# A vision tower on one Trainium2 core: value matmuls grouped, the weighing merged, PSUM banks and step orders reassigned, and the second norm applied by GpSimd

## What is computed

```
tokens  = patches(14 x 14) @ W.T + b           # 196 tokens of 128
h       = concat(token, tokens) + pos          # S = 197 rows
x       = layernorm(h)
h       = h + decayed linear attention(x)      # out[t] = sum_{s<t} LR * DECAY^(t-1-s) (q_t.k_s) v_s, @ Wo
x       = layernorm(h)
route   = argmax(softmax(relu(mean_s(x) @ r_w1 + r_b1) @ r_w2 + r_b2))   # one of 3 weight sets per image
q, k, v = x @ wq, x @ wk, x @ wv               # 8 heads of 16; 8, 4 or 1 heads of k and v
h       = h + softmax(q k.T / 4) v @ wo
```

## Time and profile before

| | |
|---|---|
| median of 3 runs | 851.34 us (851.13 to 852.95) |
| the profiled execution | 847.72 us |
| its span | 846.0 us |
| TensorE matmuls busy | 790.8 us, 93% |
| VectorE busy | 602.5 us, 71% |
| ScalarE busy | 597.9 us, 71% |
| GpSimd busy | 310.6 us, 37% |
| HBM traffic over the span | 44 GB/s |

### The profile page before, as it was taken

How to read it: one execution, slowest core, us unless ns; L and a number is a source line. 1 busy time by engine, 2 the same in 40 slices (tenths; PEclk the granted TensorE clock), 3 DMA queues, 4 the chain that set the end, 5 groups by cost and what they waited for, 6 DMA issues and landing times.

```text
span 846.0 us, 25937 instructions
## 1 busy us (share of the span) xinstructions
PE 790.8 (93%) x8624; PEld 653.0 (77%) x8624; DVE 602.5 (71%) x1956; ACT 597.9 (71%) x1364; POOL 310.6 (37%) x840
## 2 busy tenths in 40 slices
PE   3778899999999999999999999999999999998996
PEld 3666688888888888888888888888888878876774
DVE  3246777778777786878677777777777777777771
ACT  3556587777777877777787778777777777665664
POOL 1466442443344334433433343343434333431100
PEclk9899999999999999999999999999999999999998
DMA  5555645554545555455455544554455555323220
GB/s 141 149 147 157 197 144 163 155 151 140 170 144 150 147 168 161 130 155 163 146 147 161 161 142 144 169 154 141 145 162 157 146 151 154 98 67 119 95 90 20
DMA packets 138705, 120.55 MB, mean 142 GB/s; under 512 B 12606, under 2 KB 138446, under 8 KB 138574
## 3 DMA queue, kind: packets, MB, share of 16 engines
q1 hardware_dynamic: 136898, 118.34, 47.7%
q10 hardware_dynamic: 1676, 0.57, 0.4%
HBM read 30.99 MB, written 6.46 MB: 44 GB/s over the span
## 4 chain that ended last, share of the span: by engine, by line
PE 71%; DVE 14%; issue 7%; SPq 2%; POOL 2%; DMA 1%; ACT 1%; ACTq 1%; POOLq 1%; DVEq 0%
PE ps L425 11%; PE ps L592 11%; PE ps L543 9%; PE ps L515 4%; DVE top L814 4%; PE ps L569 4%; PE ps L530 3%; PE ps L574 3%; PE ps L624 3%; PE ps L474 3%; PE ps L516 2%; PE ps L484 2%; PE ps L450 2%; DVE mixed L840 2%; PE ps L557 2%
## 5 line engine op out<-in xcount | busy, mean ns | idle before, releaser
L814 DVE TENSOR_REDUCE top<-ps 99x2 f32<-99x394 f32 x512 | 265.6, 560 | 131.9 <-PE ps L543 131.9
L948 ACT ACTIVATE prob<-ps 99x396 f32<-99x396 f32 x512 | 227.2, 496 | 70.2 <-PE ps L574 69.6
L886 ACT ACTIVATE packed<-img 84x686 f32<-84x686 f32 x128 | 177.6, 1394 | 0.5 <-DMA img<-in_x 0.5
L425 PE MATMUL ps<-cols,w_tok 126*128 126x196 f32 x640 | 122.8, 339 | 3.1 <-DMA cols<-packed 2.8
L363 POOL TENSOR_TENSOR var<-mv,eps 99x2 f32<-99x2 f32 x64 | 12.6, 197 | 300.3 <-DVE mv L732 299.9
L543 PE MATMUL ps<-stack 64*99 64x198 f32 x1024 | 110.5, 294 | 7.4 <-DVE top L814 4.0
L569 PE MATMUL ps<-top_rows,pick_rows 64*99 64x198 f32 x1024 | 114.3, 254 | 1.7 <-ACT prob L948 1.5
L543 PEld LDWEIGHTS ps<-stack 64*99 64x99 f32 x1024 | 64.1, 161 | 65.3 <-issue 33.7
L574 PE MATMUL ps<-stack 64*99 64x198 f32 x1024 | 113.4, 252 | 0.0
L592 PE MATMUL ps<-prob,v_ones 99*32 99x198 f32 (+1 forms) x2048 | 112.6, 337 | 0.4 <-ACT prob L948 0.4
L425 PEld LDWEIGHTS ps<-cols,w_tok 126*128 126x128 f32 x640 | 109.0, 196 | 4.3 <-DMA cols<-packed 3.4
(11 more groups left out here) (149 smaller groups left out, 1564.7 us busy)
## 6 DMA issues: line engine op xcount, KB each, us to landing
stack<-qk SPq DMA_DIRECT2D x256, 198.0 KB, 2.5
img<-in_x SPq DMA_DIRECT2D x192, 150.1 KB
cols<-packed SPq DMA_DIRECT2D x128, 160.8 KB
cols<-packed SPq DMA_DIRECT2D x64, 128.6 KB
out<-h SPq DMA_DIRECT2D x64, 49.5 KB
out<-h SPq DMA_DIRECT2D x64, 49.0 KB
w_rows<-in_L_tok_W SPq DMA_DIRECT2D x1, 294.0 KB, 3.2
sets<-in_L_ffn_wo SPq DMA_DIRECT2D x3, 64.0 KB
```

The costliest lines, as they stand in the source:

```text
L425: last = nc.tensor.matmul(ps[:, CX, 0:N * N], w_tok[0:KROWS, s, :], cols[b.ring % 2][:, :, s, :], start=(s == 0), stop=(s == STEPS - 1))
L814: nc.vector.tensor_reduce(top[:, c // 4, first:first + 2], columns, AX.X, ALU.max, negate=True).then_inc(m_read, 1)
L886: last = nc.scalar.activation(packed[b.ring % 2][:, first:end, :], img[b.ring % IMGS][:, :].rearrange("p (x w) -> p w x", w=P)[:, first:en ...
L948: nc.scalar.activation(prob[:, c, :], ps[0:T, E0 + c % 2, 0:CHUNK], ACT.Exp, scale=DK ** -0.5).then_inc(exp_done, 1)
```

## The change

1. **PSUM.** There is no bank MIX; the four working banks are CX, CY, CZ and CW. `patches`, `project_qk` and `project_out` share CY; the turned `xhat1`, z, the turned maxima and the routing share CX; `turn_patches`, `weigh`, `attend_out` and `project_v` share CZ; `scores`, the turned `xhat2`, the mix and all that follows from it up to `turn_mixed` share CW. The waits for a bank's last reader follow.
2. **`weigh`** has two products in place of three: the first covers all 198 columns.
3. **`mix_values`**: both parts stand at the head of TensorE's slot, for the image of ENDING; before, part 0 stood late in the slot of MIXING and part 1 in the middle of the next.
4. **`normalise2`** is done by GpSimd, right behind `spread2`, for all images from 7 on (those whose ADDED slot is 12 or later); in the filling slots VectorE does it.
5. **New orders** in the full slots on TensorE, VectorE and ScalarE. The filling lists, SyncE's list and GpSimd's list of steps are the same.

```diff
-        M0, E0, MIX, CX, CY, CZ = 0, 2, 4, 5, 6, 7
+        M0, E0, CX, CY, CZ, CW = 0, 2, 4, 5, 6, 7
...
                 nc.gpsimd.tensor_tensor(rstd2[:, :], var2[:, :], half[:, :], ALU.pow).then_inc(rstd2_done, 1)
+                if b.i + ADDED >= MAXED:
+                    normalise2(b)
+
+            def normalise2(b):
+                pool.wait_ge(rstd2_done, b.i + 1)
+                pool.wait_ge(turned2, b.i)
+                for t in range(2):
+                    last = nc.gpsimd.tensor_scalar(xhat2[:, t, :], h1[b.ring][:, t, :], mv2[:, t, 0:1], rstd2[:, t:t + 1],
+                                                   ALU.subtract, ALU.mult)
+                last.then_inc(norm2_done, 1)
...
             def turn_patches(b):
                 pe.wait_ge(h0t_ready, b.i + 1)
...
+                added = b.back(ADDED - PATCHED)
+                if added.exists():
+                    pe.wait_ge(h1_ready, added.i + 1)
...
             def scores(b):
                 pe.wait_ge(z_ready, b.i + 1)
...
+                ended, added = b.back(ENDING - TURNED), b.back(ADDED + 1 - TURNED)
+                if ended.exists():
+                    pe.wait_ge(mixed_t_ready, ended.i + 1)
...
             def weigh(b):
                 pe.wait_ge(att_ready, b.i + 1)
+                topped, patched = b.back(TOPPED - TURNED), b.back(PATCHED - TURNED)
+                if topped.exists():
+                    pe.wait_ge(v_ready, topped.i + 1)
...
-                nc.tensor.matmul(ps[:, CY, 0:T], xhat[:, 0, :], att[:, 0:T], start=True, stop=True)
-                nc.tensor.matmul(ps[:, CY, T:SP], xhat[:, 0, :], att[:, T:SP], start=True, stop=False)
-                nc.tensor.matmul(ps[:, CY, T:SP], xhat[:, 1, :], att[:, SP:SP + T],
+                nc.tensor.matmul(ps[:, CZ, 0:SP], xhat[:, 0, :], att[:, 0:SP], start=True, stop=False)
+                nc.tensor.matmul(ps[:, CZ, T:SP], xhat[:, 1, :], att[:, SP:SP + T],
                                  start=False, stop=True).then_inc(u_done, 1)
...
             def turn_normed2(b):
                 pe.wait_ge(norm2_done, b.i + 1)
...
-                if ended.exists():
-                    pe.wait_ge(mixed_ready, ended.i + 1)
...
+                if turned.exists():
+                    pe.wait_ge(att_ready, turned.i + 1)
...
             def mix_values(b, g):
                 if g == 0:
...
                     pe.wait_ge(v_ready, b.i + 1)
-                    if b.has(1):
-                        pe.wait_ge(mix_ready, b.i)
+                    last_added = b.back(ADDED + 1 - ENDING)
+                    if last_added.exists():
+                        pe.wait_ge(x2t_ready, last_added.i + 1)
...
             def project_out(b):
...
+                projected = b.back(PROJECTED - ENDING)
+                if projected.exists():
+                    pe.wait_ge(lo_ready, projected.i + 1)
...
# TensorE, full slots
-                    (max_scores, maxed, 0), (key_scores, mixing, 0),
-                    (turn_top, topped), (turn_normed1, turned), (attend_out, added), (patches, patched),
...
+                    (mix_values, ending, 0), (mix_values, ending, 1), (key_scores, mixing, 0),
+                    (max_scores, maxed, 0), (turn_normed1, turned), (attend_out, added), (row_mix, ending),
...
# VectorE, full slots
+                    (maximum, maxed, 0), (maximum, maxed, 1), (choose, choosing), (normalise, ending),
+                    (add_attention, added), (maximum, maxed, 2), (maximum, maxed, 3), (tokens, patched),
+                    (mask_scores, turned), (maximum, maxed, 4), (maximum, maxed, 5), (route_relu, routing),
+                    (measure, patched), (low_halves, projected), (maximum, maxed, 6), (maximum, maxed, 7),
+                    (route_bias, routing), (finish, ending), (split_top, maxed),
...
# ScalarE, full slots
+                    (keep_mix, ending), (exponent, mixing, 0), (keep_x1t, turned), (exponent, mixing, 1),
+                    (keep_z, turned), (pack, arrived, 0), (keep_h0t, patched), (keep_mixed_t, ending),
+                    (exponent, mixing, 2), (exponent, mixing, 3), (top_row, topped), (exponent, mixing, 4),
+                    (exponent, mixing, 5), (high_halves, projected), (keep_v, topped), (keep_x2t, added),
+                    (exponent, mixing, 6), (exponent, mixing, 7), (keep_u, turned), (pack, arrived, 1),
+                    (route_exp, routing),
```

More of the change, by code:

```diff
@@ L500, in route_logits @@
                 for j in range(BATCH):
[L501 to L502 removed]
+                    last = nc.tensor.matmul(ps[0:1, CX, j * len(KV):(j + 1) * len(KV)], hidden[:, j:j + 1], r_w2[:, :],
                                             start=True, stop=True)
@@ L633, in slot @@
                 plan = [
-                    (max_scores, maxed, 0), (key_scores, mixing, 0),
-                    (turn_top, topped), (turn_normed1, turned), (attend_out, added), (patches, patched),
-                    (project_z, turned), (mix_values, ending, 1),
-                    (max_scores, maxed, 1), (key_scores, mixing, 1),
-                    (turn_patches, patched), (scores, turned), (row_mix, ending), (route_hidden, routing),
-                    (max_scores, maxed, 2), (key_scores, mixing, 2),
-                    (turn_normed2, added), (project_v, topped), (route_logits, routing), (turn_mixed, ending),
-                    (weigh, turned), (mix_values, mixing, 0),
-                    (max_scores, maxed, 3), (key_scores, mixing, 3),
-                    (project_qk, projected), (project_out, ending),
+                    (mix_values, ending, 0), (mix_values, ending, 1), (key_scores, mixing, 0),
+                    (max_scores, maxed, 0), (turn_normed1, turned), (attend_out, added), (row_mix, ending),
+                    (project_z, turned), (patches, patched), (turn_mixed, ending), (max_scores, maxed, 1),
+                    (key_scores, mixing, 1), (turn_top, topped), (scores, turned), (turn_patches, patched),
+                    (max_scores, maxed, 2), (key_scores, mixing, 2), (project_qk, projected),
+                    (route_hidden, routing), (project_v, topped), (max_scores, maxed, 3), (key_scores, mixing, 3),
+                    (turn_normed2, added), (route_logits, routing), (weigh, turned), (project_out, ending),
                 ]
@@ L852, in slot @@
                 choosing = n.back(ROUTED + 1) if n.back(ROUTED + 1).ring % BATCH == 0 else Image(-1, 0)
[L853 to L858 removed]
+                plan = [
+                    (maximum, maxed, 0), (maximum, maxed, 1), (choose, choosing), (normalise, ending),
[3 more added lines that the diff above has]
+                    (route_bias, routing), (finish, ending), (split_top, maxed),
+                ]
                 if n.i < MAXED:
```

191 lines of the change are left out of this document (90 added, 101 removed).

## The result

| | before | after |
|---|---|---|
| median of 16 runs each | 851.77 us (848.33 to 854.14) | 846.95 us (841.88 to 852.20) |
| ratio | | 0.994 (95% interval 0.9921 to 0.996) |
| the profiled execution, its span | 847.72, 846.0 us | 848.21, 846.5 us |

What follows compares the result with a forecast made beforehand. The kernel was taken as bound by the order on TensorE. Full slots -26.5, first slots -3 and last slots +14 sum to -15.5: 832.2 us profiled, 835.8 as a median, said as 835, range 825 to 847.

Steps and rivals of the forecast that it cites:

- A full slot: Slots 15 to 67: wait 0.33, weighing 0.11 and value matmuls 0.14 us gained per slot; -26.5 us over 52 slots.
- the 0.05 a slot for small waits: Full slots: allowance for small waits from thin slacks in the new order, 0.05 us a slot, between 0 and 0.3.
- the three slacks: Full slot's laid-out order: three margins no larger than a handoff's scatter, such as 0.1 to 0.2 us before group 2.
- The GpSimd pair: Full slots: `normalise2`'s two halves on GpSimd take 0.9 us together, at a cost taken as 0.
- the slack of 2.7 us: Full slot: `xhat2` from GpSimd is ready at 7.4 us, while `turn_normed2` comes at 10.1.
- The last slots, +14: Slots 67 to 78: TensorE waits for `mixed` and before score groups with little cover; +14 us, bounds 6 and 18.
- The first slots, -3: Filling slots put at 0, bounds -1 and +3; slots 13 and 14 lose waits, -3 us (0 to -5).
- The start, 0: Start to `turn_normed1` of slot 4: no change in time, 0 us.
- From profile to median, +3.6: Timed median 851.3 us lies 3.6 above the profiled execution's 847.7; 3.6 added at the end.
- Rival 1: Full slots: groups 2 and 3 each miss by 0.1 to 0.15 us per slot, +10 us: 845; chance 0.19.
- Rival 2: Last slots cost only +6 us and no small waits arise (-2.6): 825; chance 0.15.
- Rival 3: Full slots: GpSimd's new pair holds VectorE up, at `tokens` or the mask; 859 at half the pair; chance 0.07.

Runs made afterwards that it cites:

- the kernel with the filled waits: The change plus four unused products of 198 columns ahead of `turn_mixed` in slots 70 to 77: 839.78 us, ratio 0.9863 to the kernel before.
- the new orders of the last slots: The change with own step lists from slot 69: 832.93 us; mended version: 832.07 us; that plus bank E0 for `turn_patches` and `tokens` in filling slots: 830.12 us.

## Why the prediction was right and where it was wrong

The forecast for the profiled execution was 832.2 us; it took 848.2. The step that failed is the last slots: what the waits there do to TensorE's clock was put at nothing. The first slots were priced wrongly as well. The 16 us between forecast and execution, by its own steps:

- **A full slot**: right. 12.00 to 11.42 was forecast and 11.44 measured; with routing 12.25 and 12.23; -26.5 and -27.8 in all, since the 0.05 a slot for small waits did not arise. The parts of the 0.58 are not as separate as the sum has them: alone in the old order the weighing gives its 0.11, the other two nothing. Weighing (0.56 for 0.55) and value block (1.49 to the next group) are as worked out. The layout holds too: `turn_normed1` 2.22 us behind the value block, `turn_mixed` 5.32, group 1 5.59, `turn_normed2` 10.13. None of the three slacks that were "no larger than the scatter" failed.
- **The GpSimd pair**: priced wrongly. "0.9 for two halves, taken from L373, the same operation and shape" was 1.57; the operation was another, subtract-multiply, not multiply-add. (The terms of that sum also add up to 7.2, not 7.4.) GpSimd became 88 us busier, not 51. It cost nothing: it came out of the slack of 2.7 us. VectorE lost 23 us, not 28: the pair itself gave back 34.0 (38.2 to 4.2) and `chance` 4.5, but the two operations that split the maxima took 8.9 more, 5.9 of it the subtraction. (These rows add up to 29.6; the rest is not traced.)
- **The last slots, +14**: this is the step that failed; +23.7 was measured. The waits were right, slot by slot up to 77, as the kernel with the filled waits shows (+14.1). The term left out that the clock falls behind these waits, and the upper bound of 18 held nothing for it: 9.5 us. The trace of before had signs of it: its clock is at half in four stretches of 3.4 us among the waits of the first 15 slots, and from 840.7 us to the end, behind waits of 0.37 and 0.62 us and during one of 0.81 in the last slot. Between them it is whole.
- **The first slots, -3**: measured +2.3 from slot 4 to 15, so 5.3 of the 16 are here. "VectorE's own chain of that slot is as long" was wrong: without the wait for the new bank the filling slots are some 2 us shorter. In slots 12 to 14 the expected gain did not come (+0.8 for -3). `turn_normed1` stands 2 us into the slot now, and in these short slots it waits for GpSimd's `xhat1` (0.53 and 0.78 us). Whether that is all of it stays open.
- **The start, 0**: +2.2 in the profiled execution, its scatter.
- **From profile to median, +3.6**: before was profiled in one of its shortest executions, after in one 1.3 above its median. That gave back 4.9 of the 16. It was luck, and it is why 846.95 still lies inside the range of 825 to 847.

Rival 1 (small waits) gave the time, 845, for a wrong reason: TensorE waits 0.4 us in all the full slots. Rival 2's cheaper tail is not this change's, but it is possible: the new orders of the last slots get 13 to 19 of the 24 us back (tails of 108.6, 105.6 and 102.9 us; the last two have the same order). Rival 3 did not occur: `tokens` took 424 ns on average after and 416 before. The splitting of the maxima was held up instead; no wait of the full slots comes from it.

## What to carry to other kernels

When a pipeline runs dry, price each new wait of TensorE twice: by its length, and by the clock that falls behind it (here 14 and 7 to 9.5 us). Give the draining slots an order of their own, or put unused products into the wait. Moving an operation off an engine brings the step behind it forward only as far as that step's other input allows. And before costing an operation on GpSimd by another row, see that its pair of operations is the same, not only its shape.

## What the runs showed of the hardware

- TensorE's granted clock fell to its lower level (1.2 GHz) in the last slots of the change, behind waits of 1.15 to 2.23 us; slots 71 to 75 have one of 1.15 and one of 0.44 each, and it fell in four of these five. With 1.3 us of unused products in the place of the longer wait, and the 0.44 left, it stayed at 2.4 GHz up to 826.9 us, and the program was some 7 us shorter.
- GpSimd's subtract-multiply with two scalars per partition took 0.795 us on 99 x 128 float32 values, its multiply-add 0.448.
- VectorE's subtraction of 99 x 32 values took 0.205 us on average in the kernel before, and 0.67 (406.83 to 407.50) beside GpSimd's addition `kept` (406.73 to 407.46) in the kernel with `normalise2` on GpSimd alone. The Trainium skill, SBUF — State Buffer, section SBUF: two separate sides, has it that an operation with two SBUF inputs waits for one of GpSimd's that reads SBUF; these rows agree.
